# Decoder layer on one core: maxima placed into the score operands by DMA, context loaded in slots, half-precision output projections, masked probabilities cleared by GpSimd

## What is computed

```
x = layernorm(x + self_attention(x))          # latents of rank 64 (k, v) and 128 (q), 16 heads,
                                              # q and k are 16 content + 32 rotary features, causal
x = layernorm(x + (cross_attention(x, ctx, ctx) @ W.T + b))   # 16 heads of 16 features,
                                              # keys and values are the raw context, no projection
x = layernorm(x + top2_of_8_experts(x))       # gate, W1 (256x1024), exact gelu, W2 (1024x256)
scores = q k^T * scale; masked to -inf above the diagonal in self_attention only; softmax over keys
```

## Time and profile before

| | |
|---|---|
| median of 3 runs | 706.69 us (705.56 to 711.62) |
| the profiled execution's own time | 706.66 us |
| its span, first to last instruction | 704.8 us, mean granted clock of TensorE 0.964 |
| first phase | start to about 440 us |
| experts | about 440 to 678 us |
| last norm and stores | 678 to 704.8 us |

### The profile page before, as it was taken

One profiled execution on the slowest core, in us unless ns is written; L12 is line 12 of the kernel. 1 busy time (PEld: TensorE's weight loads), 2 busy tenths in 40 slices (PEclk: granted clock), 3 DMA queues, 4 the chain that ended last, 5 costly groups with the idle time before them and its releaser, 6 DMA issues.

```text
span 704.8 us, 22698 instructions
## 1 busy us (share of the span) xinstructions
PE 610.6 (87%) x8063; PEld 447.7 (64%) x8064; DVE 517.4 (73%) x1106; ACT 397.3 (56%) x847; POOL 292.9 (42%) x245
## 2 busy tenths in 40 slices
PE   2678989999999999999886797899999999999940
PEld 1456756676676667667564556678777777777720
DVE  5797898997786878677677986867666666666635
ACT  4335668767568484866778693554434444444414
POOL 3688574436264641543111012233444444444422
PEclk9789999999999999999999997999999999999985
DMA  8435253240322304304344045122222222222226
GB/s 276 151 103 151 78 166 91 63 121 6 111 69 72 82 1 119 110 21 118 106 121 136 1 119 180 19 32 46 47 47 45 45 45 45 44 45 39 43 40 223
DMA packets 39839, 59.45 MB, mean 84 GB/s; under 512 B 6768, under 2 KB 27504, under 8 KB 39632
## 3 DMA queue, kind: packets, MB, share of 16 engines
q1 hardware_dynamic: 32272, 48.12, 23.3%
q0 software_dynamic: 7488, 10.23, 8.9%
HBM read 34.08 MB, written 11.67 MB: 65 GB/s over the span
## 4 chain that ended last, share of the span: by engine, by line
PE 34%; DVE 11%; DMA 6%; ACT 4%; issue 4%; POOL 2%; ACTq 1%; SPq 1%; DVEq 1%; POOLq 0%
PE bank L1688 6%; PE bank L1690 3%; DVE mxc L1085 3%; DMA x_sb<-x_rows,slot_row 2%; PE scores L1678 2%; PE bank L1678 2%; PE scores L1680 2%; PE scores L1679 2%; PE bank L1292 2%; DMA acc_rows<-x,slot_row 2%; PE bank L1680 2%; PE bank L1679 2%; POOL acc_rows L627 1%; ACT probs L742 1%; PE scores L1343 1%
## 5 line engine op out<-in xcount | busy, mean ns | idle before, releaser
L742 ACT ACTIVATE probs<-scores 128x768 f32<-128x768 f32 (+1 forms) x128 | 114.3, 918 | 51.0 <-PE scores L1349 40.2
L627 POOL DMA_INDIRECT acc_rows<-x,slot_row x39 | 65.2, 1671 | 132.7 <-DVE x L1198 129.8
L1688 PE MATMUL bank<-w_sb,wp 128*128 x312 | 109.9, 380 | 1.9 <-DVE wp L1185 1.9
L1085 DVE TENSOR_REDUCE mxc<-scores 128x4 f32<-128x1024 f32 x64 | 76.5, 1217 | 20.4 <-PE scores L1363 19.8
L1690 PE MATMUL bank<-w_sb,wp 128*128 x312 | 85.1, 273 | 0.0
L813 ACT ACTIVATE probs<-scores,b_sb 128x128 f32<-128x128 f32 x160 | 45.5, 368 | 63.3 <-PE scores L1680 63.3
L813 ACT ACTIVATE probs<-bank,b_sb 128x128 f32<-128x128 f32 x152 | 43.4, 370 | 65.6 <-PE bank L1680 65.6
L1183 DVE CAST wp<-probs 128x512 f16<-128x512 f32 x78 | 36.1, 462 | 60.3 <-ACT probs L813 59.8
L1050 DVE TENSOR_REDUCE mx<-scores 128x6 f32<-128x768 f32 x64 | 59.8, 950 | 15.7 <-PE scores L1331 15.2
L1678 PE MATMUL scores<-xT,w_sb 128*128 128x128 f16 x320 | 61.2, 223 | 2.2 <-DVE xT L909 1.2
L1679 PE MATMUL scores<-xT,w_sb 128*128 128x128 f16 x320 | 61.2, 223 | 0.0
(11 more groups left out here) (267 smaller groups left out, 1712.1 us busy)
## 6 DMA issues: line engine op xcount, KB each, us to landing
w_sb<-w_sb SPq DMA_DIRECT2D x192, 64.0 KB, 2.4
wstage<-in_w_exp SPq DMA_DIRECT2D x16, 512.0 KB
w_sb<-in_w_exp SPq DMA_DIRECT2D x8, 512.0 KB, 5.3
wp<-in_w_exp SPq DMA_DIRECT2D x8, 512.0 KB, 4.2
x_sb<-in_x_by_feature SPq DMA_DIRECT2D x8, 256.0 KB, 3.5
ctx_raw<-in_ctx SPq DMA_DIRECT2D x8, 256.0 KB, 3.1
x_res<-in_x SPq DMA_DIRECT2D x8, 256.0 KB, 3.5
x_rows<-x SPq DMA_DIRECT2D x8, 256.0 KB, 3.1
```

The costliest lines, as they stand in the source:

```text
L627: nc.gpsimd.indirect_dma_start(out=acc_rows[:, :], out_offset=bass.IndirectOffsetOnAxis(ap=slot_row[:, n:n + 1], axis=0), in_=yb[n % 2], i ...
L742: nc.scalar.activation(probs[:, 2 * (k % 4):2 * (k % 4) + 2, 0:cols], ps_p[pair[u, k, b]][:, :, 0:cols], ACT.Exp, scale=(SELF_SCALE, CROSS ...
L1085: nc.vector.tensor_reduce(mxc[:, 2 * k:2 * k + 2, :], ps_p[pair[u, k, b]][:, :, :].rearrange("p h (a k) -> p h a k", a=2), axis=AX.X, op=A ...
L1688: mm(o[:, 0:2 * D], ah[:, u, f, :], weights(e, at, 2 * D), start=(f == 0), stop=(f == FC - 1), skip_group_check=True)
```

## The change

1. **The maxima.** The matmuls of lines 1346 and 1358 are gone. `negm` and `mT` are float16 and hold -maximum/64. After DVE's copy to `mT`, SP moves the 16 rows of `mT` with two DMAs into a free row of each head's slot of the query operand (`mq` into `qk16`, `mr` into `xs`); the key operand holds 64 in the same row, so the score product itself subtracts the maximum. `se` and `ce` now wait for these DMAs (`max_moved`).
2. **The mask.** The matmuls of line 1349 are gone too. After ACT's exponential, POOL sets the masked probabilities of each unit to zero (`ec`, affine_select over 128 x 2 x 2 x 128 values, eight a batch), and `sv` waits for POOL and not for ACT. The mask matmuls of `sm` stay.
3. **The context.** A transposed copy of the context is a new input. Per batch SP loads it (`ci`, 256 KB), ACT and POOL split it (`cx`: one ACT and one POOL instruction, where ACT had two), SP stores both parts to device memory (`cp`, 256 KB) and loads them back in slots (`cq`, six DMAs of 64 KB, into two buffers in turn). `st` transposes only x: two units of 8 transposes a batch instead of four, two ACT copies instead of four.
4. **Output projections.** `wo` and `wx` are split into float16 parts once. `sb` and `cb` now have a DVE instruction as well (low part of `oT`, 128x512 from PSUM), and `sw` and `cw` are 12 float16 matmuls of 128x256 in place of 4 in float32.
5. **Orders.** All strings are new, several PSUM banks are assigned anew, the store of GpSimd's DMA descriptors is halved (8192 to 4096), and DVE sets two more stretches of `qk16` at the start.

The core of the diff (the order strings are told below by their rows):

```
-                for part in range(12):
+                pe.wait_ge(m_mv[0], b * 32 + 32)
+                for part in range(6):
                     for h in (2 * k, 2 * k + 1):
                         last = self_exp_part(h, part, b)
...
-                pe.wait_ge(a_p[0], b * (H // 2) + 2 * k + 2)
+                pe.wait_ge(p_p, b * (H // 2) + 2 * k + 2)
                 weighted_values(k, v_sb, True)
...
+            elif u in ("move_self_max", "move_cross_max"):
+                a = 0 if u == "move_self_max" else 1
+                sp.wait_ge(v_mT[a], b + 1)
+                for r in range(2):
+                    row = (RD, P - RD - HD)[r] if a == 0 else QK * r + 3 * HD
+                    to = qk16[row:row + 1, :, 0, 0:T] if a == 0 else xs[row:row + 1, :, :]
+                    sp.dma_start(to, mT[a][QK * r:QK * r + H // 2, :]).then_inc(m_mv[a], 16)
...
+            elif u == "clear_late_keys":
+                pool.wait_ge(a_p[0], b * (H // 2) + k + 1)
+                diag = probs[:, 2 * (k % 4):2 * (k % 4) + 2, :].rearrange("p h (a t) -> p h a t", a=2)[:, :, :, 0:P]
+                nc.gpsimd.affine_select(diag, diag, [[0, 2], [0, 2], [1, P]], ALU.is_ge, 0.0, base=0,
+                                        channel_multiplier=-1).then_inc(p_p, 1)
...
             def cross_exp_part(h, t, b):
-                if part % 2 == 0:
-                    return mm(s, xc[rows, hp, 1, t * P:(t + 1) * P], xc[rows, hp, 0, :], start=True, stop=False)
-                return mm(s, ident_b[rows, r + hp:r + hp + 1].broadcast_to([QK, P]), mT[1][rows, :], start=False, stop=True)
+                return mm(s, cs[b % 2][rows, hp, t * P:(t + 1) * P], xs[rows, hp, :], start=True, stop=True)
...
+            elif u == "load_context_slots":
+                sp.wait_ge(c_pt, b * 16 + 16)
...
+                for slot in range(3):
+                    heads = c_parts[b, slot // 2].rearrange("(g r d) t -> r d g t", r=2, d=HD)
+                    for r in range(2):
+                        row = QK * r + HD * slot
+                        sp.dma_start(cs[b % 2][row:row + HD, :, :], heads[r]).then_inc(c_sl[b % 2], 16)
...
+            elif u in ("self_back", "cross_back"):
+                dve.wait_ge(a_n2[a], b + 1)
...
+                nc.vector.tensor_tensor(oTl, ps_back[a][:, :].rearrange("p (c t) -> p c t", c=DC), oTh, ALU.subtract).then_inc(v_bl[a], 1)
...
             def project_heads(a, w):
                 for t in range(TT):
                     for c in range(DC):
-                        last = mm(ps_out[a][:, t * D:(t + 1) * D], oT[:, c, t * P:(t + 1) * P], w[:, c, :],
-                                  start=(c == 0), stop=(c == DC - 1))
+                        for i, (left, part) in enumerate(((oTh, 0), (oTl, 0), (oTh, 1))):
+                            last = mm(ps_out[a][:, t * D:(t + 1) * D], left[:, c, t * P:(t + 1) * P], w[:, part, c, :],
+                                      start=(c == 0 and i == 0), stop=(c == DC - 1 and i == 2))
...
-    nc = bacc.Bacc("TRN2", target_bir_lowering=False, num_devices=1, dynamic_dma_scratch_size=8192)
+    nc = bacc.Bacc("TRN2", target_bir_lowering=False, num_devices=1, dynamic_dma_scratch_size=4096)
```

415 lines of the change are left out of this document (219 added, 196 removed), and 2 rows, old and new, of the table UNITS.

## The result

The changed kernel is slower: 719.0 us median of four runs (714.4 to 721.1) against 706.3 (705.6 to 711.6), a ratio of 1.0155 with a 95% interval of 1.0083 to 1.0226. The forecast was 687 us, range 665 to 706. The profiled execution, 714.41 us with a span of 712.7, was the quickest of the four, so its rows show some 5 us less of the loss than the median.

What follows compares the result with a forecast made beforehand. The prediction took TensorE to set the steady stretch's pace, VectorE close behind and longest after the change. From 706.7 us: -23.6 (steady stretch), +1 (fill), +2.5 (drain) = 686.6, so 687 us, range 665 to 706.

Steps and rivals of the forecast that it cites:

- What TensorE loses: Steady stretch: removed or cheaper matmuls save TensorE 6.8 us a batch, 47.6 us in seven batches, from 278.7 to 231.1.
- What the others gain: Steady stretch: VectorE's work rises to 247.5 us, ScalarE's falls to 188, GpSimd's rises to 192 with clears at 1.2.
- added lock between VectorE and GpSimd: Steady stretch: GpSimd's added work may hold up VectorE instructions with two SBUF inputs; 0 to 13 us, 3 taken.
- The steady stretch after: First to last self residual add: VectorE becomes longest, 90% full, so 275 us against 298.6, 23.6 us less.
- new waits take it: Rival, steady stretch: waits stop VectorE 3 us more per batch, gain falls to 2.6; 704 to 708 us, chance 0.11.
- Fill +1: Up to the first self residual add: maxima's DMA, first clear and start memset, less TensorE work; +1 us, -2 to +5.
- Drain +2.5: Last self to last cross residual add: maxima's DMA and low parts of `oT` lengthen it; +2.5 us, -2 to +6.
- Experts: Expert phase after the attention: TensorE nearly full, its instructions unchanged, so its 237.6 us are carried over.
- SP has room: SP's DMA queue: 12 more issues a batch, 7.5 us, on some 33 or 21 us in about 39 us, fit.
- GpSimd as the bound: Rival, steady stretch: clears above 2.0 us make GpSimd longest, about 740 us at 2.5; with a stopped queue, chance 0.09.

Runs made afterwards that it cites:

- b_nomask: Kernel before, with the mask matmuls of the self exp left out and nothing in their place: 707.1 us.
- b_nomax: Kernel before, with the maxima's matmuls of the self and cross exps left out and no DMA in their place: 706.9 us.
- b_less: Kernel before, with VectorE's maxima taken over half of each block's keys: 698.1 us.
- b_nomm_less: Kernel before, with maxima over half of each block's keys and the exps' mask and maxima matmuls left out: 693.5 us.
- e4_no_moves: Changed kernel without the DMAs that move the maxima, so their subtraction is left out: 712.0 us.
- a_noclear: Changed kernel without GpSimd's clears, the weighted sums waiting for ScalarE's exp: 721.1 us.
- e2b: Changed kernel, with the two start memsets of the scale rows done by GpSimd instead of VectorE: 725.2 us.
- b_clear: Kernel before, with the self exp's mask matmuls left out and GpSimd clearing the masked probabilities, the weighted sums waiting for it: 727.3 us.
- b_proj: Kernel before, with only the output projections changed to two half-precision parts (12 fp16 matmuls instead of 4 fp32): 727.1 us.
- b_both2: Kernel before, with half-precision projections and GpSimd's clears, projections and weighted sums both placed later in TensorE's order: 753.8 us.
- b_proj2: Kernel before, with half-precision projections, each placed up to two units later in TensorE's order: 730.3 us.
- b_max: Kernel before, with only the maxima moved by DMA from SyncE in place of their matmuls, mask matmuls kept: 735.1 us.

## Why the prediction was wrong, step by step

*What TensorE loses: right.* A self_exp unit takes 0.51 us (241.29 to 241.80 in the timeline) against 0.84 in the earlier trace rows, 0.50 expected. A projection takes 1.32 us from its start to the next unit's (215.72 to 217.04), as expected. TensorE's work in the stretch fell by 42 us at full clock, 47.6 expected. That 246.4 us remained busy and not 231 is mostly the low clock: 12.3 of the 15.3 us.

*What the others gain: right or too high.* VectorE 238.3 (247.5 forecast), ScalarE 188.8 (188), GpSimd 159.8 (192), since a clear takes 0.70 us and not 1.2. The added lock between VectorE and GpSimd, priced at 3 us, did not come for line 1056, now 1105: median 1.48 us for the shape of the earlier trace rows, 1.91 before.

*The steady stretch after: this step failed.* "The longest engine is now VectorE at 247.5 us ... I take 90%: 247.5 / 0.90 = 275 us." VectorE is 81% full. The stretch took 292.7 us instead of 275: 17.7 of the 27.4 us by which the profiled run missed the forecast, the fill another 8.1. A ratio of busy time to length, read in one stretch, was used as if the longest engine's work drove the length. b_nomask, b_nomax, b_less and b_nomm_less show that it doesn't: 19 us of TensorE work are worth 1.3 to 4.7 us of the whole, 46.4 us of VectorE work are worth 10, and 23 us of TensorE and 47 us of VectorE work together 14.7. TensorE's 93% was no proof that it set the pace. The account that fits all four: the engines run fixed orders and hand buffers to each other, so a unit that ends earlier finds the next wait where the order put it. The chain of waits itself was not followed from end to end.

*The rival "new waits take it" was the mechanism.* In the steady stretch its size was near: it asked for 3 us a batch on VectorE and left a gain of 2.6 us; TensorE's idle time rose by 26.5 us, 3.8 a batch, and 5.8 us were gained. Its 704 to 708 us for the kernel was too low since it kept the fill of the forecast. Which waits it would be was open: alone, each part opens waits of 9 to 24 us in the stretch, but in the changed kernel the new orders cover most of them (e4_no_moves: some 7 us for the moves; a_noclear: none for the clears). The largest that is left, 10.1 us behind the merged counters, belongs to none of the parts that the prediction priced.

*Fill +1: failed, +9.1.* The range ended at +5. TensorE's first matmul comes at 11.78 us, in before at 7.37; VectorE's two new memsets ahead of it take 3.5 us, where the prediction had them in words but not in the sum. e2b took them off VectorE, and the first matmul still came 3 us later than in before. Alone, the clears make the fill 7.1 us longer than b_nomask, the maxima 3.7 longer than b_nomax, the context 4.6 longer than before, the projections 0.5. Undoing one of them in the changed kernel brings nothing back (a_noclear 88.3, e4_no_moves 87.9, e2b 88.0). That several causes each suffice is what this suggests; which one would be last was not settled.

*Drain +2.5: right, +3.4.* *Experts: right.* *SP has room: right on average* (189 issues in the steady stretch of before, 27 a batch and not 33), *wrong in the pause shown above*, where six issues in a row stood ahead of the two moves that a merged counter made one cast wait for.

*GpSimd as the bound: fell*, at 0.70 us a clear.

*What I had not considered: the clock.* Behind TensorE's pauses the granted clock was at its lower level (1.2 GHz): 0.51 in the mean from 30 to 47 us, behind a pause of 2.71 us that ended at 30.22, and 0.55 from 383 to 397, behind one of 3.19 that ended at 386.24. By the rows of the stretches it takes 0.14 x 54.7 = 7.7 us of TensorE's time in the fill (4.7 before), 12.3 in the steady stretch (2.8) and 0.13 x 38.1 = 5.0 in the drain (0). The Trainium skill ("TensorE: Matmul & The Clock Gate", section "HAM oscillation — how this bites in real kernels") describes waits that throttle the array again and again; the trace agrees, with seven such stretches between 97 and 344 us where before has one. What it costs the kernel is not shown. These 17.5 us more of TensorE's time are an estimate of its direct part, and they are more than the 12.7 us that the kernel lost, so the clock stays a rival for the loss against before. In b_clear, b_proj and b_both2 idle time grew by 16 to 42 us and the time that the low clock takes by 3 to 8, so there it is not the larger part. No variant of the changed kernel keeps the clock up without added work.

## What to carry to other kernels

Before pricing work taken from an engine, ask the chip what such work is worth: leave it out with nothing in its place. Two such runs (b_nomask, b_nomax) would have turned this forecast from -20 us to about none. Where all engines run written orders, busy shares near 90% on one engine don't make it the bound, and a part that moves work to another engine must be priced by the wait that it puts ahead of the next unit, which moving one engine's order alone handed on in b_proj2. Compare a part with its own removal (b_clear with b_nomask, b_max with b_nomax): the difference is the price of the way in which it is done. And read the whole diff for waits that an edit widens: a counter shared by two kinds of transfer makes every reader wait for both.
